# Position attention: where the row maxima are taken off, and who begins their transfer

## The reference, cut to what matters

```python
def _L1_xattn_ref(q, k, v, gamma):          # B,Dq,Lq = 64,64,256: tokens are the "channels"
    qh = q.reshape(B, 8, 8, 256); kh = k.reshape(B, 8, 8, 256); vh = v.reshape(B, 8, 8, 256)
    qk = jnp.einsum('bhdq,bhdl->bhql', qh, kh) * 8 ** -0.5
    sm = jax.nn.softmax(qk, axis=-1)
    return gamma * jnp.einsum('bhql,bhdl->bhdq', sm, vh).reshape(B, 64, 256)
x = _layernorm(x + _L1_xattn_ref(x, ctx_2048, ctx_2048, L1_xattn_gamma))
```

## Time and profile before

| | |
|---|---|
| median of three runs | 5089.75 us |
| the profiled execution's own time | 5091.97 us |
| its span, first to last instruction | 5090.2 us |
| mean granted TensorE clock | 0.961 of full speed |
| PE / DVE / ACT / POOL busy over the span | 4538.3 / 3297.4 / 2040.4 / 1518.0 us |
| the section: its first memset, its first matmul, its last instruction | 864.68, 903.01, 1546.33 us |
| in 1160 to 1260 us: PE / DVE / ACT / POOL busy | 96.89 / 74.42 / 48.63 / 32.90 of 100 us |

### The profile page before, as it was taken

How to read it: one execution, slowest core, us unless ns; L and a number is a source line. 1 busy time by engine, 2 the same in 40 slices (tenths; PEclk the granted TensorE clock), 3 DMA queues, 4 the chain that set the end, 5 groups by cost and what they waited for, 6 DMA issues and landing times.

```text
span 5090.2 us, 89514 instructions
## 1 busy us (share of the span) xinstructions
PE 4538.3 (89%) x33622; PEld 3195.2 (63%) x33669; DVE 3297.4 (65%) x6372; ACT 2040.4 (40%) x4326; POOL 1518.0 (30%) x3018
## 2 busy tenths in 40 slices
PE   8988997899997988888379999999997999999788
PEld 6766886566665667776246666666664666666455
DVE  5657236677776757878755555555554666666798
ACT  4544113354553433333135445455542434334222
POOL 1111005333321223333234344334432322222122
PEclk9999998899998999999589999999998999999999
DMA  1012000333320000000100000000001000000000
GB/s 42 2 51 61 1 6 31 79 78 75 77 57 32 1 8 8 7 8 7 67 30 1 1 1 1 1 1 1 1 1 56 9 7 9 8 8 6 5 14 16
DMA packets 114779, 111.54 MB, mean 22 GB/s; under 512 B 20848, under 2 KB 107056, under 8 KB 109872
## 3 DMA queue, kind: packets, MB, share of 16 engines
q1 hardware_dynamic: 114352, 105.82, 8.0%
HBM read 89.00 MB, written 16.78 MB: 21 GB/s over the span
## 4 chain that ended last, share of the span: by engine, by line
PE 50%; DVE 19%; issue 15%; POOL 9%; DMA 4%; ACT 3%; SPq 2%; POOLq 0%; DVEq 0%; ACTq 0%
PE banks L2246 13%; PE banks L2489 4%; PE banks L727 4%; POOL factors L2696 3%; PE banks L1761 3%; DMA stack<-parts_x 3%; PE banks L2312 2%; PE banks L1172 2%; PE banks L754 2%; DVE neg_max L1085 1%; PE banks L1671 1%; PE banks L2410 1%; POOL rstd L265 1%; PE banks L2338 1%; PE banks L499 1%
## 5 line engine op out<-in xcount | busy, mean ns | idle before, releaser
L263 POOL TENSOR_TENSOR var_eps<-mean_var,ln_eps 128x1 f32<-128x1 f32 x384 | 83.1, 216 | 1635.5 <-DVE mean_var L259 1091.3
L1085 DVE TENSOR_REDUCE neg_max<-banks 128x2 f32<-128x512 f32 x512 | 343.4, 682 | 191.4 <-PE banks L1075 184.8
L1202 ACT ACTIVATE exps<-banks 128x512 f32<-128x512 f32 x512 | 304.7, 597 | 309.1 <-PE banks L1156 292.3
L2300 DVE TENSOR_TENSOR q_normed<-banks,factors 128x512 f32<-128x512 f32 x256 | 176.4, 689 | 230.5 <-POOL factors L2290 230.5
L2267 ACT ACTIVATE squares<-banks 128x512 f32<-128x512 f32 x256 | 153.1, 598 | 411.6 <-PE banks L2246 411.6
L2290 POOL TENSOR_TENSOR factors<-mean_squares,minus_half 128x4 f32<-128x4 f32 x256 | 258.0, 1008 | 21.6 <-POOL mean_squares L2286 0.5
L2672 ACT ACTIVATE squares<-q_normed 128x512 f32<-128x512 f32 x160 | 100.8, 630 | 396.0 <-DVE q_normed L2662 396.0
L1075 PE MATMUL banks<-stack,stack 128*128 128x256 bf16 x1024 | 202.6, 281 | 63.3 <-DMA stack<-parts_x 57.7
L1761 PEld LDWEIGHTS banks<-yT,w_swiglu 128*128 128x128 f32 x2048 | 238.5, 193 | 30.2 <-issue 29.9
L1761 PE MATMUL banks<-yT,w_swiglu 128*128 128x128 f32 x2048 | 247.4, 277 | 8.5 <-DVE hidden L1785 8.5
L1155 PE MATMUL banks<-stack,stack 128*128 128x256 bf16 x1024 | 253.1, 274 | 1.6 <-ACT exps L1202 1.2
(11 more groups left out here) (381 smaller groups left out, 11140.0 us busy)
## 6 DMA issues: line engine op xcount, KB each, us to landing
contextT<-in_ctxT SPq DMA_DIRECT2D x96, 128.0 KB, 2.5
parts_context<-parts SPq DMA_DIRECT2D x96, 64.0 KB, 2.0
parts_x<-parts SPq DMA_DIRECT2D x96, 64.0 KB, 2.0
stack<-parts_context SPq DMA_DIRECT2D x32, 192.0 KB
stack<-parts_x SPq DMA_DIRECT2D x32, 192.0 KB
x_all<-in_x SPq DMA_DIRECT2D x1, 4096.0 KB, 14.1
context<-in_ctx SPq DMA_DIRECT2D x64, 64.0 KB, 2.2
context<-in_ctx SPq DMA_DIRECT2D x32, 128.0 KB, 2.3
```

What stands on the lines that cost most here:

```text
L1085: v.tensor_reduce(self.mx[s][:, :, g:g + 1], self.bM[g % 2].rearrange("p (h c) -> p h c", h=DH), AX.X, ALU.max, negate=True).then_inc(self ...
L1202: self.nc.scalar.activation(self.e[n % 8][:], self.bE[n % 2].rearrange("p (l c) -> p l c", l=DH), ACT.Exp, scale=self.TOK ** -0.5).then_in ...
```

## The change

The maxima no longer get their own matmul. The three rows of `neg_maxT` that belong to a head are moved into rows 96 to 98 of the query stack, and rows 96 to 127 of the key stack are set to 1.0 once, so that the score matmul itself, over all 128 rows, takes the maxima off. The maxima pass now reads rows 0 to 95 only. ScalarE begins the three transfers (`move_max_act`), one tick behind the copy, and the first score of a tile waits for them. With this, scores start at tick 10; a `weigh` is cut in two halves of 16 matmuls that stand two ticks apart, the last at tick 13; the maxima banks hold two heads each (four banks) and VectorE reduces two heads in one instruction; the turned maxima use a slot of the score banks; the reciprocal is cut in two, and the output pieces move to lag 6.

```diff
-    STEP, SCORES_FROM = 16, 6
+    STEP, SCORES_FROM, TURN_AT = 16, 10, 4
+    ROWS, MAX_ROWS = 96, 128
...
     def setup_pool(self, pool):
         for i in (0, 1):
             for n in range(self.STACK_BUFFERS):
-                pool.memset(self.kq[i][n][:].bitcast(I32), 0)
+                last = pool.memset(self.kq[i][n][:].bitcast(I32), 0)
+        last.then_inc(self.zeroed.sem, 1)
+        pool.wait_ge(self.zeroed.sem, self.zeroed.at(1))
+        for n in range(self.STACK_BUFFERS):
+            last = pool.memset(self.kq[0][n][self.ROWS:self.MAX_ROWS], 1.0)
...
     def max_dve(self, dve, t, s):
-        for g in range(self.HEADS):
-            dve.wait_ge(self.made.sem, self.made.at(t, g + 1))
...
+        for i in range(8):
+            yield
+            dve.wait_ge(self.made.sem, self.made.at(t, i + 1))
...
+            v.tensor_reduce(self.mx[s][:, :, 2 * i:2 * i + 2].rearrange("p h g -> p g h"), self.bM[i % 2].rearrange("p g (h c) -> p g h c", h=DH),
+                            AX.X, ALU.max, negate=True).then_inc(self.maxed.sem, 1)
...
+    def move_max_act(self, act, t, s):
+        for _ in range(self.TURN_AT + 1):
+            yield
+        act.wait_ge(self.m_copied.sem, self.m_copied.all(t))
+        for j in range(3):
+            act.dma_start(self.stack(1, t)[self.ROWS + j:self.ROWS + j + 1, :, :],
+                          self.mT[s][32 * j:32 * j + self.HEADS, :]).then_inc(self.m_moved.sem(t), 16)
...
     def score(self, pe, t, s, n):
         if n == 0:
-            pe.wait_ge(self.m_copied.sem, self.m_copied.all(t))
+            pe.wait_ge(self.m_moved.sem(t), self.m_moved.all(t))
...
         for l in range(DH):
-            out = self.bE[n % 2][:, l * D:(l + 1) * D]
-            self.nc.tensor.matmul(out, k[:, h, l * P:(l + 1) * P], q[:, h, :], start=True, stop=False)
-            last = self.nc.tensor.matmul(out, self.sel[:, h, :], self.mT[s][:], start=False, stop=True)
+            last = self.nc.tensor.matmul(self.bE[self.slot(t, n) % 2][:, l * D:(l + 1) * D], k[rows, h, l * P:(l + 1) * P], q[rows, h, :], start=True, stop=True)
...
+    def weigh_at(self, pe, t, s, tick):
+        r, after = divmod(tick - self.SCORES_FROM - 5, 4)
+        if 0 <= r < 4 and after % 2 == 0:
+            self.weigh(pe, t, s, r, after // 2)
...
-            "pool": [(3, self.values_pool), (5, self.tail_pool), (1, self.split_pool)],
+            "pool": [(3, self.values_pool), (6, self.tail_pool), (1, self.split_pool)],
```

More of the change, by code:

```diff
@@ L1117, in copy_max_act @@
     def copy_max_act(self, act, t, s):
-        for _ in range(4):
+        for _ in range(self.TURN_AT):
             yield
@@ L1165, in weigh @@
                 pe.wait_ge(self.o_read.sem, self.o_read.all(t - 2))
-        for part in range(4):
-            l, ones = divmod(part, 2)
+        for ones in (0, 1):
             for g in range(4):
@@ L1171, in weigh, with score_from_pe, score_late_pe, weigh_last_pe @@
                 out = self.bO[s][32 * g:32 * g + 32, ones * D:(ones + 1) * D]
-                last = self.nc.tensor.matmul(out, left, self.e[n % 8][:, l, :], start=(r == 0 and part == 0),
+                last = self.nc.tensor.matmul(out, left, self.e[n % 8][:, l, :], start=(r == 0 and l == 0 and ones == 0),
                                              stop=(r == 3 and l == DH - 1), skip_group_check=True)
-        last.then_inc(self.weighed.sem, 1)
-    def score_pe(self, pe, t, s):
-        for tick in range(self.STEP):
-            if tick >= self.SCORES_FROM:
+        if l == DH - 1:
+            last.then_inc(self.weighed.sem, 1)
+    def weigh_at(self, pe, t, s, tick):
+        r, after = divmod(tick - self.SCORES_FROM - 5, 4)
+        if 0 <= r < 4 and after % 2 == 0:
+            self.weigh(pe, t, s, r, after // 2)
+    def score_pe(self, pe, t, s):
+        for tick in range(self.SCORES_FROM, self.STEP):
+            self.score(pe, t, s, tick - self.SCORES_FROM)
+            self.weigh_at(pe, t, s, tick)
+            yield
+    def score_from_pe(self, pe, t, s):
+        for _ in range(self.SCORES_FROM):
+            yield
+        yield from self.score_pe(pe, t, s)
+    def score_late_pe(self, pe, t, s):
+        for tick in range(self.STEP, 2 * self.STEP):
+            if tick - self.SCORES_FROM < self.HEADS:
                 self.score(pe, t, s, tick - self.SCORES_FROM)
-            for r in range(4):
-                if tick == self.SCORES_FROM + 4 * r + 5:
-                    self.weigh(pe, t, s, r)
+            self.weigh_at(pe, t, s, tick)
             yield
-    def score_late_pe(self, pe, t, s):
-        for tick in range(self.STEP):
-            n = tick + self.STEP - self.SCORES_FROM
-            if n < self.HEADS:
-                self.score(pe, t, s, n)
-            for r in range(4):
-                if tick + self.STEP == self.SCORES_FROM + 4 * r + 5:
-                    self.weigh(pe, t, s, r)
+    def weigh_last_pe(self, pe, t, s):
+        for tick in range(2 * self.STEP, 2 * self.STEP + 2):
+            self.weigh_at(pe, t, s, tick)
             yield
@@ L1218, in out_dve @@
         v = self.nc.vector
-        for _ in range(9):
+        yield
+        yield
+        dve.wait_ge(self.weighed.sem, self.weighed.all(t))
+        for half in (0, 1):
+            at = slice(half * P, (half + 1) * P)
+            v.reciprocal(self.rd[:, at], self.bO[s][:, D + half * P:D + (half + 1) * P]).then_inc(self.o_read.sem, 1)
             yield
-        dve.wait_ge(self.weighed.sem, self.weighed.all(t))
-        v.reciprocal(self.rd[:], self.bO[s][:, D:2 * D]).then_inc(self.o_read.sem, 1)
+            yield
+        dve.wait_ge(self.o_read.sem, self.o_read.at(t, 2))
+        v.scalar_tensor_tensor(self.on[s][:], self.bO[s][:, 0:D], self.gamma[:, 0:1], self.rd[:], ALU.mult, ALU.mult).then_inc(self.o_read.sem, 1)
         yield
-        dve.wait_ge(self.o_read.sem, self.o_read.at(t, 1))
-        v.scalar_tensor_tensor(self.on[s][:], self.bO[s][:, 0:D], self.gamma[:, 0:1], self.rd[:], ALU.mult, ALU.mult).then_inc(self.o_read.sem, 1)
         yield
```

77 lines of the change are left out of this document (47 added, 30 removed).

## The result

The changed kernel takes 5193.53 us (median of four runs, 5188.02 to 5197.46) against 5088.07 us (5085.45 to 5090.58): 1.021 times the time before, 95% interval 1.019 to 1.022. It is 105 us slower. The forecast was 5100 us with a range to 5130, so sign and size are both to be explained: slower had a chance of 0.45, but no case in the forecast reached this far.

The account below looks back on a forecast made before the run. PE's pace and the PE, POOL, DMA, PE loop (2 x 19.4 us) bound it almost equally. Fourteen loops of 39.3 us plus start and drain ended 3.9 us earlier; memsets of 14.5 made +10.6 on 5089.75, rounded 5100 us; range 5064 to 5130.

Parts of the forecast that it names:

- Cost zero, with the four ticks between as cover, about 1 us of it unused: ScalarE's three transfers of the maxima: land 2.0 us after issue, at about 8 us, before the first score at 9.45.
- this rival: Transfers of the maxima land late beside the stack reads: 2 us of delay adds 28 us, 5129 us; chance 0.15.
- The loop through the last `weigh`: GpSimd's values copy waits for the last weigh at tick 13, making a loop of 37.1 us, 39.3 with slow clock.
- The cold clock: PE idles 5.4 us before every other step, the clock halves behind it, and 2.2 us of work are lost.
- Writes of parts, 3.3 us: In the loop, from GpSimd's split until the writes have landed and the stack reads are issued: 3.3 us.
- PE's pace: PE's own work per step in the changed kernel: 15.4 us, or 16.3 for a step directly following another.
- Memsets: Four GpSimd memsets at the section's start, timed by elements: 3.62 us each, 14.5 us in all, hidden by nothing.
- VectorE: Reductions of 1024 elements take 1.22 us each, half a reciprocal 0.95 us, all within VectorE's idle time.
- Start and drain: Section's ends: third stack lands at 931.4 before memsets are added; step 34's start to the last output takes 43.2 us.

Follow-up runs that it names:

- e1: Changed kernel with the three transfers written to a spare tile and the first score waiting only for ScalarE's copy, maxima not taken off: 5116.25 us.
- e7: Changed kernel without any transfers of the maxima, so maxima not taken off and the first score waiting only for ScalarE's copy: 5112.57 us.
- e4: Kernel before the change with GpSimd's pieces in the order split, tail, values: 5084.17 us, ratio 0.9991.
- e3: Changed kernel with the stack rows reordered so each stack read has 8 as its slowest dimension: 5039.75 us, ratio 0.9903.
- e2: Changed kernel with GpSimd's pieces in the order split, tail, values: 5035.05 us, ratio 0.9895.
- e6: Changed kernel's new order and memsets, but maxima still taken off by the matmul with select and nothing moved by ScalarE: 5136.98 us, ratio 1.0094.

## Why the prediction was wrong

The step that failed is "Cost zero, with the four ticks between as cover, about 1 us of it unused", the moves. I took 2.0 us from issue to landing, the row of a transfer that nothing stood in front of. The runs show 7.3 to 9.7 us from the first issue in every other step, a wait of 3.4 us on the mean at the first score (34.1 / 10), and 77 us that come back when nothing waits for the moves (e1). I had written down this rival, with the right place, the right reason and even the nearest row, `contextT` at 10.0 us behind the same reads the earlier trace rows. It got 0.15 and a price of 2 us. Two things were wrong in that weighing.

- *The price.* The ends of the range for a landing were 2.0 and 10.0 us. I took the lower because the moves are on another queue and small. The runs show that neither helped here: they landed about 8.5 us after the first issue where stack reads were ahead. The upper row would have put the landing 10.0 us behind the issues at 4.8 to 6.0, at 14.8 to 16.0, against a first score at 9.45: 5 to 7 us of wait, above the 3.4 measured but much nearer to it than nothing.
- *The chance.* Whether they meet is a question of phase, and the forecast had all the terms for it. A step that waits begins at 0, the other loop's step at 17.6; its stack reads are issued 12.9 + 0.4 + 7.5 + 3.3 = 24.1 us later, at 41.7, which is 2.4 us into the next waiting step (39.3), and land at 15.4. The moves of that step are issued between 4.8 and 8 us. Moves that land with the reads at 15.4 would have held up a first score due at 9.45 + 2.2 = 11.65 by some 4 us. The two meet in each loop, and not by chance; measured, the reads are issued 3.65 us into the step (1218.36 and 1222.01). For the other step the same sum puts the reads behind the moves, and there the trace has no wait.

Point by point, by the prediction's own steps:

- *The loop through the last `weigh`*: right. GpSimd waits for it in each step, PE waits for every other stack, and in the kernel without late moves the loop is 40.5 us against the 39.3 forecast. Of the kernel before, though, the 33 waits that led me to it are 18: the rows of PE and of PEld are the same waits seen twice.
- *The cold clock*: right as to place. In the section after 930 us PE has 27 idle pieces of 2 us or more that begin at the full clock, and in or just behind 26 of them the clock falls. I counted one such piece for each loop; late moves made it two. Of the 77 us of e1 the waits themselves are 51.6. The other 26 fit the clock behind them: the loop's first piece is on the mean 5.2 us longer than in e1 (21.9 against 16.7), 1.8 more than the mean wait of 3.4, and in the one loop where the clock held it is 2.9 longer, with a wait of 3.2. No run holds the clock up with the moves late, so the share of the clock is worked out and not shown by itself.
- *Writes of parts, 3.3 us*: 4.65 in the loop shown, but 3.3 in more than half of the section's steps and 3.8 on the mean of the 13 loops, so some 0.5 x 14 = 7 us lie here. It is not the moves: e7, which has none, takes 3.7 on the mean and is longest at the same tiles (5.4 and 4.7 us), and the kernel before has stretches of 4.2 to 4.5. Why they are longer stays open.
- *PE's pace*: 15.4 to 16.3 us forecast, 17.00 measured where nothing else waits. A half round and the gap ahead of it take 1.09 us and not 1.035 (1202.53 + 0.22 to 1203.84 below, 0.4 a step), and the wait of 0.62 us for ScalarE's copy was not in the sum at all; smaller gaps make up the rest. It lengthens the loop too, by some 1 us ahead of tick 13, which is most of what e1 (40.5) has over the forecast (39.3).

```profile
1202.53 0.38 PE L1193 MATMUL banks<-stack,stack 128*128 128x256 bf16 x2
1202.84 0.64 PE L1208 MATMUL banks<-exps,values 128*32 128x256 f32 x8
1203.29 0.61 PE L1208 MATMUL banks<-exps,ones 128*32 128x256 f32 x8
1203.84 0.39 PE L1088 MATMUL banks<-stack,stack 96*128 96x256 bf16 x2
```

- *Memsets*: 13.9 us against 14.5, by elements: right.
- *VectorE*: right to 0.01 us, 1.221 for a reduction and 0.944 for half a reciprocal:

```profile
L1100 DVE TENSOR_REDUCE neg_max<-banks 128x4 f32<-128x1024 f32 x256 | 312.0, 1221 | 307.5 <-PE banks L1088 307.3
...
L1270 DVE RECIPROCAL rden<-banks 128x128 f32<-128x128 f32 x64 | 60.2, 944 | 12.3 <-PE banks L1208 12.3
```

- *Start and drain*: 8 us short. The turn of step 5 comes at 955.82 and not at 931.4 + 14.5 + 4.6 = 950.5, and from the turn of step 34 to the end it is 41.5 us and not 38.6. The first move wait alone is 6.59 us, at 946.22, where PE has nothing else to do.

The missing 93 us are therefore 85 in the 29 steps between those turns (652.4 measured, 567.8 by the sum), and 8 at the two ends. That part was also read wrongly in one more place: I gave PE in the kernel before a need of 18.5 us, and 0.9 us a step to the loop. With the loop taken out it still needs 19.14 (e4).

## What to carry to other kernels

The time of a new small transfer depends on what is ahead of it: here three moves of 8 KB were in 3 to 5 us after the first issue with nothing in the way, and 7 to 10 us behind the stack reads, though another queue began them. Work out when in the loop the big transfers are under way, and price the small one by the nearest row that met them; if a rival has such a row and the forecast's case has not, the rival is the forecast. And when work is taken off an engine that shares a loop with others, look in the list of each in-order engine for the piece that now waits for the latest event, and ask whether anything behind it could stand in front: here that was one line, worth 158 us.

## What the runs showed of the hardware

- The shape of a transfer counts beside its size. Six reads a tile of the same bytes took 13.2 us with 3, 2 and 8 as slowest dimensions and 9.5 with 8 in all (e3).
- A small transfer on ScalarE's queue got no way past large ones on SyncE's. Three moves of 8 KB were in 7.3 to 9.7 us after the first issue where stack reads were ahead of them and 3.1 to 5.0 us where not; the median of one was 3.6 us in the changed kernel and 2.0 in e2, where they are issued ahead of the reads.
- GpSimd's memset goes by elements: 3.47 us for 32 x 4096 bf16 and 1.76 us for the same bytes as 32 x 2048 int32 (7.04 us for four), close to the 1.81 us of 128 x 2048 int32, so between 32 and 128 partitions the number does not count.
- A kernel whose PE runs without a long break at 20.38 us a step (e6) was 57 us faster than one whose PE needs only 17.00 but idles: 26 of the 27 idle pieces, 2.1 to 5.8 us long, took the clock down as well.
